# Queries and keys turned one row tile at a time in three self-attentions of a twelve-layer kernel

## The chip, the core and the metric

The kernel runs on one core of one Trainium2 chip, as one program of 42,986 instructions. The metric is the device time of a run in microseconds (us). Before the change three runs gave 1915.62, 1916.70 and 1917.58 us, median 1916.7.

## The reference, cut to what matters

The model has four blocks of cross-attention, self-attention and feed-forward over x (32 batches of 32 rows, 256 wide). Each layer gets a layer norm of x and is added to x. Three of the four self-attentions are touched; q, k and v have 16 heads of 16 columns, and a batch attends only within itself:

```python
# L0: softmax with a causal mask, interleaved rotation
q, k = rope(x @ W_Q), rope(x @ W_K)
out  = softmax(where(causal, q @ k.T / 4, -inf)) @ v @ W_O
# L2: 4 key/value heads; RMS norm of each head, then rotation, scores capped
q, k = rope(rms(x @ w_q)), rope(rms(x @ w_k))
out  = softmax(where(causal, 50 * tanh(q @ k.T / 4 / 50), -inf)) @ v @ w_o
# L3: sigmoid instead of softmax, heads of q and k divided by their length
q, k = l2norm(xn @ Wq), l2norm(xn @ Wk)          # xn: a second layer norm of x
out  = (sigmoid(15 * (q @ k.T - 0.29514)) * gate_q * gate_k) @ v @ Wo + bo
```

## The kernel before, in words

The 1024 rows are 8 row tiles of 128 (`NT = 8`), four batches each; 256 columns are two chunks of 128 (`C = 2`). Everything is float32. `PS` is PSUM, 8 banks of 512 columns. Layers run one after another; each is a block of five instruction streams, and each engine executes its own stream strictly in the written order, waiting on semaphores. The three stages are `l0_self` (line 2044, "softmax", tiles named l0a), `l2_self` (line 3398, "capped", l2a) and `l3_self` (line 3947, "resonance", l3a). All use the class `SelfAttention` (line 374).

**Preparation.** PE projects tile t to queries and keys (bank 4 + t % 2, line 419) and to values (bank 6 + t % 2, line 430). ACT copies them out (`copy_projections`, lines 501 and 488), and in l2a and l3a also writes squares (line 505) and takes the roots of their sums (line 496). DVE sums the squares (line 536), normalises and rotates: lines 760, 761, 771, 772 in l0a; 3461, 3463, 760, 761, 777, 778, 782, 783 in l2a; 4048, 4049, 4051 in l3a, where POOL multiplies by gates (line 4006) and DVE sums and applies them to the values (lines 4055, 4058).

**Turning.** `turn_tensor` transposes queries and keys of four row tiles into banks 0 to 3, one bank for each of two query and two key chunks. After each half ACT copies three banks (`turn_scalar`, lines 472 and 475) and DVE one (`turn_vector`, line 483), 512 columns at a time; keys are written twice, multiplied by one of two column masks. The second half waits until both have copied the first, since it uses the same banks. `keep_busy` (line 95) issues products of constants into bank 6 while PE would wait; their number is in `IDLE`.

**Attention.** Only then does `attend_tensor` start. For each row tile t:

- compare: PE, 64 instructions of 32 rows, scores to banks 0 to 3 (line 562). It waits until the scores of tile t - 1 have been read.
- softmax: DVE adds the mask and takes tops (lines 692, 698), POOL subtracts (673), ACT takes the exponential (628). capped: ACT tanh (622) and exponential (628), POOL masks (678). resonance: ACT sigmoid (634), POOL multiplies by a gate (678).
- DVE transposes the weights (714, `turn_probs`), ACT (and POOL) spread the values (615, 665), PE weighs them (576) into bank 4 + t % 2, DVE inverts and normalises (702, 708) or ACT copies (640), DVE transposes the rows (718, `turn_rows`), PE projects (585) into bank 6 or 7 by pairs of tiles, DVE adds each pair to X (737) and takes its moments.

PE's order is compare(t + 1), weigh(t - 1), proj(t - 2) for t = 0 to 9.

Of the kernel before, what the change touches and what calls it, by code (L numbers as in the profile page):

```python
# [14 lines left out]
ALU = mybir.AluOpType  # L15
# [3 lines left out]
P = 128  # L19
# [3 lines left out]
C = D // P  # L23
# [347 lines left out]
IDLE = {"l0a": (0, 0, 0, 0, 3, 0, 2, 0, 3), "l2a": (0, 0, 1, 3, 4, 2, 2, 2, 3), "l3a": (0, 0, 0, 0, 12, 0, 0, 3, 5)}  # L371


class SelfAttention:
# [10 lines left out]
    def __init__(self, core, es, name, kind, scale, kv_heads=16):  # L385
        self.core, self.name, self.kind, self.scale = core, name, kind, scale
        self.kv_heads, self.heads, self.width = kv_heads, 16 + kv_heads, (16 + kv_heads) * 16
        self.idle = IDLE[name]
# [15 lines left out]
        self.turned, self.half_copied_act, self.half_copied_dve = sem("turned"), sem("half_copied_act"), sem("half_copied_dve")  # L404
# [28 lines left out]
    def turn_tensor(self, pe, half):  # L433

        nc, PS = self.core.nc, self.core.PS
        if half:
            pe.wait_ge(self.v_copied, NT - 1)
            self.core.keep_busy(6, self.idle[4])
            pe.wait_ge(self.half_copied_act, 1)
            pe.wait_ge(self.half_copied_dve, 1)  # L440
        for t in range(4 * half, 4 * half + 4):
            if t % 4 and self.idle[t]:
                pe.wait_ge(self.v_copied, NT - 1)
                self.core.keep_busy(6, self.idle[t])
            pe.wait_ge(self.qk_rows, t + 1)
            for n, rows in enumerate((self.Q, self.K)):
                for c in range(C):
                    last = nc.tensor.transpose(PS[:, 2 * n + c, (t % 4) * P:(t % 4 + 1) * P], rows[:, t, c * P:(c + 1) * P], self.core.ident[:])
                    if t % 4 == 3:
                        last.then_inc(self.turned, 1)  # L450

    def project_tensor(self, pe, xT, wqk, wv):
# [8 lines left out]
        self.turn_tensor(pe, 0)  # L461
        self.turn_tensor(pe, 1)

    def half_of_keys(self, c, half, side):
        return self.K2[:, c, half * (B // 2):(half + 1) * (B // 2), side, :]

    def turn_scalar(self, act, half, side_of):

        nc, PS = self.core.nc, self.core.PS
        for c in range(C):  # L470
            act.wait_ge(self.turned, 4 * half + c + 1)
            nc.scalar.copy(self.QT[:, c, half * 512:(half + 1) * 512], PS[:, c, :])
        act.wait_ge(self.turned, 4 * half + 3)
        for side in range(2):
            last = nc.scalar.activation(self.half_of_keys(0, half, side), PS[:, 2, :].rearrange("p (b k) -> p b k", k=S), ACT.Copy, scale=side_of[:, side:side + 1])
        last.then_inc(self.half_copied_act, 1)

    def turn_vector(self, dve, half, side_of):

        nc, PS = self.core.nc, self.core.PS  # L480
        dve.wait_ge(self.turned, 4 * half + 4)
        for side in range(2):
            last = nc.vector.tensor_scalar(self.half_of_keys(1, half, side), PS[:, 3, :].rearrange("p (b k) -> p b k", k=S), side_of[:, side:side + 1], None, ALU.mult)
        last.then_inc(self.half_copied_dve, 1)
# [5 lines left out]
    def copy_projections(self, act, side_of, squares=None, size=None, second_half=None, values_from=0, **root):  # L490
# [7 lines left out]
        for t in range(NT):  # L498
# [14 lines left out]
            if t == NT - 2:  # L513
                self.turn_scalar(act, 0, side_of)
        if squares is not None:
            roots(NT - 1)
        self.turn_scalar(act, 1, side_of)
# [33 lines left out]
    def attend_tensor(self, pe, wo):  # L551
# [3 lines left out]
        def compare(t):  # L555
            if t:
                pe.wait_ge(self.scores_read, t)
# [22 lines left out]
        def proj(t):  # L580
            pe.wait_ge(self.out_copied, t + 1)
            if t % 2 == 0 and t >= 4:
                pe.wait_ge(self.added, t // 2 - 1)
# [10 lines left out]
        for t in range(NT + 2):  # L594
# [4 lines left out]
            if t >= 2:  # L599
                proj(t - 2)  # L600

    def attend_scalar(self, act, batch_of, gated=None):
# [39 lines left out]
        if self.kind == "capped":  # L642
            cap(0)
# [3666 lines left out]
```

## Time and profile before

| | |
|---|---|
| median of three runs | 1916.7 us (1915.62 to 1917.58) |
| the profiled execution | 1916.3 us, its span 1914.5 us |
| PE busy | 1792.7 us, 94% of the span |
| DVE, ACT, POOL busy | 1049.4, 847.6, 555.5 us |
| chain that ended last, by engine | PE 75%, DVE 11%, DMA 5%, issue 4%, ACT 3% |
| `keep_busy` of the whole kernel (line 95) | 320 records, 81.8 us on PE |

A page of the profile shows one execution. PE is the tensor engine's matrix products, PEld its weight loads, DVE, ACT and POOL are the vector, scalar and GpSimd engines. "PEclk" is the granted clock of the tensor engine as a share of 2.4 GHz. PE's busy time includes the products of `keep_busy`. A float32 product appears as two records or as four where it has two chunks.

### The profile page before, as it was taken

The numbers are of one execution on the slowest core, as the hardware profiler recorded it, in microseconds if no ns is written. First come the engines' busy times: TensorE is split into PE (matmuls) and PEld (weight loads), VectorE is DVE, ScalarE is ACT, GpSimd is POOL, SyncE is SP. The second block draws the span as 40 slices with busy tenths as digits, with TensorE's granted clock in tenths as the row PEclk, the third lists the DMA queues.
The fourth block names the chain that finished last, engine by engine and source line by source line (L and its number), as shares of the span: only waits on it lengthen the run. The fifth ranks groups of instructions, "written<-read, shape, count | busy, mean of one in ns | idle before, by whom it ended". The sixth has DMA issues, their size and how long they took to land.

```text
span 1914.5 us, 42986 instructions
## 1 busy us (share of the span) xinstructions
PE 1792.7 (94%) x16790; PEld 1384.6 (72%) x16790; DVE 1049.4 (55%) x2665; ACT 847.6 (44%) x2411; POOL 555.5 (29%) x596
## 2 busy tenths in 40 slices
PE   8999889999999989899999989999799899998998
PEld 6886569844766756699999967777544577766787
DVE  7787752252366438875555545556755555447411
ACT  6664541232266344334333335555511566635332
POOL 4441133100254203301222113332202465514242
PEclk9999889999999999999999999999999999998899
DMA  4221069570124110051899642111011455300397
GB/s 150 53 62 43 13 243 324 192 237 29 26 49 121 37 56 3 25 202 64 306 330 335 246 135 85 48 50 60 4 56 60 111 155 154 100 1 2 125 347 251
DMA packets 88303, 234.02 MB, mean 122 GB/s; under 512 B 10176, under 2 KB 45664, under 8 KB 81600
## 3 DMA queue, kind: packets, MB, share of 16 engines
q1 hardware_dynamic: 78416, 210.61, 33.0%
q0 software_dynamic: 5664, 15.47, 2.5%
q10 hardware_dynamic: 4048, 5.52, 0.9%
q8 instruction: 120, 1.97, 0.4%
q14 instruction: 55, 0.45, 0.1%
HBM read 216.35 MB, written 12.07 MB: 119 GB/s over the span
## 4 chain that ended last, share of the span: by engine, by line
PE 75%; DVE 11%; DMA 5%; issue 4%; ACT 3%; POOL 1%; SPq 0%; ACTq 0%; POOLq 0%; PEldq 0%; DVEq 0%; PEld 0%
PE PS L1137 15%; PE PS L1606 6%; PE PS L1148 5%; PE PS L3682 3%; PE PS L3502 3%; PE PS L3186 3%; PE PS L3707 3%; PE PS L3194 3%; PE PS L2402 2%; PE PS L2459 2%; PE PS L2761 2%; PE PS L2443 2%; PE PS L3219 2%; DMA l1x_probsT<-in_ctx_dram 2%; PE PS L2473 1%
## 5 line engine op out<-in xcount | busy, mean ns | idle before, releaser
L2361 POOL TENSOR_TENSOR l1x_probs<-l1x_probs,l1x_total 128x512 f32<-128x512 f32 x64 | 68.4, 1070 | 208.7 <-DVE l1x_total L2609 208.6
L1606 PE MATMUL PS<-weights,l0x_ctxT 128*128 128x256 f32 x512 | 121.0, 387 | 0.0
L1137 PE MATMUL PS<-l1f_xT,l1f_slot 128*128 128x128 f32 x1024 | 117.0, 275 | 0.0
L1137 PEld LDWEIGHTS PS<-l1f_xT,l1f_slot 128*128 128x128 f32 x1024 | 115.7, 192 | 0.1
L1606 PEld LDWEIGHTS PS<-weights,l0x_ctxT 128*128 128x128 f32 x512 | 94.6, 191 | 14.8 <-issue 2.1
L3156 POOL TENSOR_TENSOR l2x_probs<-l2x_probs,l2x_total 128x512 f32<-128x512 f32 x64 | 65.0, 1038 | 129.7 <-DVE l2x_total L3352 129.7
L95 PE MATMUL PS<-consts 128*128 128x256 f32 x320 | 81.8, 401 | 1.2
L1264 DVE SCALAR_TENSOR_TENSOR l1f_product<-PS,l1f_slot,l1f_side 128x128 f32<-128x128 f32 x128 | 36.0, 344 | 65.9 <-ACT l1f_side L1220 65.9
L3682 PE MATMUL PS<-l3x_keysT,l3x_QW 128*128 128x289 f32 x256 | 69.4, 415 | 1.7 <-issue 1.7
L95 PEld LDWEIGHTS PS<-consts 128*128 128x128 f32 x320 | 61.7, 201 | 12.3 <-issue 4.4
L1090 POOL DMA_INDIRECT l1f_out_dram<-l1f_out,l1f_sort_target_row x23 | 22.7, 986 | 159.5 <-DVE l1f_out L1247 159.5
L1220 ACT ACTIVATE l1f_side<-PS,l1f_slot 128x128 f32<-128x128 f32 x128 | 36.5, 368 | 66.0 <-PE PS L1137 66.0
L2534 ACT ACTIVATE l1x_probs<-PS,l1x_top 128x257 f32<-128x257 f32 x128 | 59.8, 475 | 6.8 <-DVE l1x_top L2604 4.4
L1786 ACT ACTIVATE l0x_sq<-PS 128x256 f32<-128x256 f32 x128 | 47.8, 385 | 33.3 <-PE PS L1606 33.2
L3707 PE MATMUL PS<-tagged,l3x_QT 128*128 128x256 f32 x256 | 60.6, 379 | 0.9 <-ACT tagged L3803 0.9
L3186 PE MATMUL PS<-l2x_ctxT,weights 128*128 128x257 f32 x256 | 61.1, 381 | 0.0
L2402 PE MATMUL PS<-HT,weights 128*128 128x512 f32 x128 | 55.9, 595 | 5.3 <-DVE l1x_AT L2572 5.3
L1137 PE MATMUL PS<-HT,weights 128*128 128x128 f32 x512 | 59.3, 276 | 1.5 <-DVE l1f_gated L1269 1.1
L3194 PE MATMUL PS<-weights,l2x_ctxT 128*128 128x256 f32 x256 | 60.4, 379 | 0.0
L1137 PEld LDWEIGHTS PS<-HT,weights 128*128 128x128 f32 x512 | 58.3, 192 | 2.7 <-DVE l1f_gated L1269 1.6
L1264 DVE SCALAR_TENSOR_TENSOR l1f_product<-PS,weights,l1f_side 128x128 f32<-128x128 f32 x120 | 33.8, 344 | 47.8 <-ACT l1f_side L1220 47.7
L3294 ACT ACTIVATE l2x_probs<-PS,l2x_top 128x257 f32<-128x257 f32 x128 | 59.2, 482 | 1.3 <-DVE l2x_top L3346 1.3
(661 smaller groups left out, 4583.7 us busy)
## 6 DMA issues: line engine op xcount, KB each, us to landing
l1f_slot<-in_experts_up_dram SPq DMA_DIRECT2D x16, 2056.0 KB, 9.9
weights<-in_experts_up_dram SPq DMA_DIRECT2D x8, 2056.0 KB, 10.2
l0f_slot<-in_experts_up_dram SPq DMA_DIRECT2D x15, 1024.0 KB, 7.9
weights<-in_experts_down_dram SPq DMA_DIRECT2D x21, 640.0 KB, 5.3
l1f_slot<-in_experts_down_dram SPq DMA_DIRECT2D x16, 640.0 KB, 4.5
l0x_ctxT<-in_ctxT_dram SPq DMA_DIRECT2D x32, 257.0 KB, 2.6
l2x_ctxT<-in_ctxT_dram SPq DMA_DIRECT2D x32, 257.0 KB, 2.7
l3x_ctxT<-in_ctxT_dram SPq DMA_DIRECT2D x32, 257.0 KB, 2.7
```

Source lines behind the costliest of these rows:

```text
L95: self.nc.tensor.matmul(self.PS[:, bank, 0:2 * P], self.ident, self.consts[:, 0:2 * P], start=True, stop=True)
L1137: done = nc.tensor.matmul(PS[:, bank + a, m * P:(m + 1) * P], mat[:, c, m * P:(m + 1) * P], x, start=(c == 0), stop=(c == 1))
L1148: done = nc.tensor.matmul(PS[:, 7, 0:D], self.hidden[j][:, m, :], w["down"][:, m, :], start=(m == 0), stop=(m == 3))
L1264: done = nc.vector.scalar_tensor_tensor(p[:, m, :], PS[:, 2 * u + 1, m * P:(m + 1) * P], w["b3"][:, 4 * u + m:4 * u + m + 1], self.side[u] ...
L1606: last = nc.tensor.matmul(PS[:, 2 * (b % 2) + k, half * D:(half + 1) * D], ctxT[b % SLOTS][:, c, half * P:(half + 1) * P], kw[:, c, k * D: ...
L2361: nc.gpsimd.tensor_tensor(p, p, bcast(total[b % 2][:, 2 * n:2 * n + 2], 2, KEYS), ALU.mult).then_inc(probs_done, 1)
L2402: done = nc.tensor.matmul(PS[:, 2 * (n % 2) + g, :], ff1[:, c, (g * HB + m) * P:(g * HB + m + 1) * P], core.HT[:, c, half * 512:(half + 1) ...
L3156: nc.gpsimd.tensor_tensor(p, p, bcast(total[b % 2][:, 2 * n:2 * n + 2], 2, 2 * P), ALU.mult).then_inc(probs_done, 1)
L3186: last = nc.tensor.matmul(PS[:, 4 + 2 * o, 0:CTX], wk[:, c, o * P:(o + 1) * P], ctxT[b % 2][:, c, :], start=(c == 0), stop=(c == 1))
L3194: last = nc.tensor.matmul(PS[:, 5, half * D:(half + 1) * D], ctxT[b % 2][:, c, half * P:(half + 1) * P], wv[:, c, :], start=(c == 0), stop ...
L3682: done = nc.tensor.matmul(PS[:, 2 * (b % 2) + u, 0:KEYS], QW[:, c, b, 4 * u:4 * u + 4, :].rearrange("p h q -> p (h q)"), keysT[b % 2][:, c ...
L3707: nc.tensor.matmul(PS[:, 6 + c, 0:2 * P], tokens[b % 2][:, half, c * P:(c + 1) * P], probsT[b % 2][:, half, :], start=(half == 0), stop=False)
```

## The change

Queries and keys are now turned one row tile at a time. All four transposes of a tile go side by side into bank 6, and ACT alone copies them out: one copy of 256 columns and two masked ones. PE turns three tiles before compare(0), ACT copies two before its attention begins. The other tiles are turned at the end of PE's turns of the attention loop, and copied at the start of ACT's. DVE prepares only `rows_ahead` tiles before its attention loop (6 in l0a, 4 in l2a and l3a) and one more at the end of each turn of the loop (`between`); in l3a POOL's gate products follow in the same way. The output projection has only bank 7, so that its next pair waits for the addition of the one before, and DVE's addition moves to the start of its turn. `keep_busy` of the turning phase is gone.

```diff
-IDLE = {"l0a": (0, 0, 0, 0, 3, 0, 2, 0, 3), "l2a": (0, 0, 1, 3, 4, 2, 2, 2, 3), "l3a": (0, 0, 0, 0, 12, 0, 0, 3, 5)}
+ROWS_AHEAD = {"l0a": 6, "l2a": 4, "l3a": 4}
+TURNS_AHEAD = 3
...
+    def turn(self, pe, t):
         nc, PS = self.core.nc, self.core.PS
+        if t == 0:
             pe.wait_ge(self.v_copied, NT - 1)
+        else:
+            pe.wait_ge(self.turn_copied, t)
+        pe.wait_ge(self.qk_rows, t + 1)
+        for n, rows in enumerate((self.Q, self.K)):
+            for c in range(C):
+                last = nc.tensor.transpose(PS[:, 6, (2 * n + c) * P:(2 * n + c + 1) * P], rows[:, t, c * P:(c + 1) * P], self.core.ident[:])
+        last.then_inc(self.turned, 1)
...
-        self.turn_tensor(pe, 0)
-        self.turn_tensor(pe, 1)
...
+    def copy_turned(self, act, t, side_of):
         nc, PS = self.core.nc, self.core.PS
+        act.wait_ge(self.turned, t + 1)
+        nc.scalar.copy(self.QT[:, :, t * P:(t + 1) * P], PS[:, 6, 0:2 * P].rearrange("p (c n) -> p c n", c=C))
+        keys = PS[:, 6, 2 * P:4 * P].rearrange("p (c b k) -> p c b k", c=C, k=S)
         for side in range(2):
+            last = nc.scalar.activation(self.K2[:, :, TB * t:TB * (t + 1), side, :], keys, ACT.Copy, scale=side_of[:, side:side + 1])
+        last.then_inc(self.turn_copied, 1)
...
         def compare(t):
+            pe.wait_ge(self.turn_copied, t + 1)
             if t:
                 pe.wait_ge(self.scores_read, t)
...
         def proj(t):
             pe.wait_ge(self.out_copied, t + 1)
-            if t % 2 == 0 and t >= 4:
-                pe.wait_ge(self.added, t // 2 - 1)
+            if t % 2 == 0 and t >= 2:
+                pe.wait_ge(self.added, t // 2)
             for c in range(C):
-                last = nc.tensor.matmul(PS[:, 6 + t // 2 % 2, ...
+                last = nc.tensor.matmul(PS[:, 7, ...
...
-        self.core.keep_busy(6, self.idle[NT])
-        pe.wait_ge(self.half_copied_act, 2)
-        pe.wait_ge(self.half_copied_dve, 2)
+        for t in range(TURNS_AHEAD):
+            self.turn(pe, t)
         pe.wait_ge(self.v_copied, NT)
         compare(0)
         for t in range(NT + 2):
...
             if t >= 2:
                 proj(t - 2)
+            if t + TURNS_AHEAD < NT:
+                self.turn(pe, t + TURNS_AHEAD)
...
+        for t in range(TURNS_AHEAD - 1):
+            self.copy_turned(act, t, side_of)
         if self.kind == "capped":
             cap(0)
         spread_values(0)
         for t in range(NT + 2):
+            if t + TURNS_AHEAD - 1 < NT:
+                self.copy_turned(act, t + TURNS_AHEAD - 1, side_of)
             if self.kind == "capped" and t + 1 < NT:
                 cap(t + 1)
...
         for t in range(NT + 3):
+            if t >= 4 and t % 2 == 0:
+                add(t // 2 - 2)
             if softmax and t < NT:
                 mask(t)
...
             if 0 <= t - 2 < NT:
                 turn_rows(t - 2)
+            between(t)
             if t >= 4 and t % 2 == 0:
                 j = t // 2 - 2
-                x = X[:, 2 * j:2 * j + 2, :]
-                dve.wait_ge(self.proj_done, 2 * j + 2)
-                nc.vector.tensor_tensor(x, PS[:, 6 + j % 2, :]...
                 dve.wait_ge(self.added, j + 1)
                 self.core.norm.take(dve, None, (2 * j, 2 * j + 1))
```

In `l2_self` DVE's preparation becomes (l3a alike, with `normalise_heads` and, one tile behind, `gate_values`; l0a has `rotate(t)` for six tiles, and the copy of the flipped second half after the third):

```diff
+            def rotate(t):
+                dve.wait_ge(at.rooted, t + 1)
+                dve_step(dve, nc.vector.reciprocal(size[:, t, :], size[:, t, :]))
...
+                rotation.products(dve, t)
+                rotation.combine(dve, t)
...
+            def between(t):
+                if t + at.rows_ahead < NT:
+                    rotate(t + at.rows_ahead)
...
+            for t in range(NT):
+                at.sum_squares(dve, t, squares, size)
+                if t % 2:
+                    rotate(t // 2)
+                elif t == 2:
                     flip.vector(dve, 1, core.HT)
```

## Rows read from the trace of the kernel before

**Rows 1.** Busy time by stretch, l2a and l3a: PE, PEld, DVE, ACT, POOL, clock, DMA.
```profile
1332.60:1398.10 65.50, 49.99 (x951) 37.69 (x950) 47.24 (x137) 38.33 (x92) 18.13 (x19) 0.94 0.10 34
1705.20:1776.50 71.30, 63.48 (x969) 44.44 (x969) 52.15 (x109) 42.65 (x94) 31.14 (x28) 0.90 0.01 2
```

**Rows 2.** Timeline of l0a: start, us, engine, line, operation, count [idle before <- releaser].
```profile
205.08 0.69 DVE L760 TENSOR_TENSOR l0a_cosines<-l0a_QK,weights 128x512 f32<-128x512 f32 x1 [0.62 <-ACT l0a_QK L501]
...
206.62 0.42 DVE L772 TENSOR_TENSOR l0a_QK<-l0a_cosines,l0a_sines 128x256 f32<-128x256 f32 x1
...
206.84 1.03 PE L430 MATMUL PS<-weights,HT 128*128 128x256 f32 x4
...
218.31 0.69 DVE L692 TENSOR_TENSOR l0a_scores<-PS,weights 128x512 f32<-128x512 f32 x1 [1.45 <-PE PS L562]
...
236.70 0.65 DVE L692 TENSOR_TENSOR l0a_scores<-PS,weights 128x512 f32<-128x512 f32 x1
...
239.32 0.69 DVE L737 TENSOR_TENSOR X<-PS,X 128x512 f32<-128x512 f32 x1
...
241.00 0.66 DVE L692 TENSOR_TENSOR l0a_scores<-PS,weights 128x512 f32<-128x512 f32 x1
...
248.07 0.45 DVE L718 STREAM_TRANSPOSE HT<-l0a_rows 128x256 f32<-128x256 f32 x1
```

**Rows 3.** Timeline of l2a.
```profile
1342.53 0.68 DVE L351 COPY HT<-PS 128x512 f32<-128x512 f32 x1
...
1349.03 0.55 PE L430 MATMUL PS<-weights,HT 128*128 128x64 f32 x4
...
1352.47 0.60 PE L448 MATMUL PS<-consts,l2a_QK 128*128 128x128 f32 x4
...
1356.20 0.26 DVE L3461 RECIPROCAL l2a_size<-l2a_size 128x20 f32<-128x20 f32 x1
...
1358.64 0.27 DVE L3461 RECIPROCAL l2a_size<-l2a_size 128x20 f32<-128x20 f32 x1
...
1368.61 0.62 ACT L628 ACTIVATE l2a_probs<-l2a_scores 128x512 f32<-128x512 f32 x1
...
1394.92 0.45 DVE L718 STREAM_TRANSPOSE HT<-l2a_rows 128x256 f32<-128x256 f32 x1
```

**Rows 4.** Timeline of l3a.
```profile
1729.22 1.03 PE L430 MATMUL PS<-weights,HT 128*128 128x256 f32 x4
...
1748.49 0.69 ACT L634 ACTIVATE l3a_probs<-PS,l3a_shift 128x512 f32<-128x512 f32 x1
...
1749.23 1.10 PE L562 MATMUL PS<-l3a_K,l3a_QT 32*32 32x64 f32 x64 [0.95 <-ACT l3a_probs L634]
...
1758.16 1.10 PE L562 MATMUL PS<-l3a_K,l3a_QT 32*32 32x64 f32 x64
...
1759.19 1.14 PE L576 MATMUL PS<-l3a_blocks,l3a_probsT 128*32 128x68 f32 x32
...
1760.26 2.08 PE L585 MATMUL PS<-weights,HT 128*128 128x256 f32 x4
...
1764.84 0.85 PE L562 MATMUL PS<-l3a_K,l3a_QT 32*32 32x64 f32 x64
...
1765.63 0.68 PE L576 MATMUL PS<-l3a_blocks,l3a_probsT 128*32 128x68 f32 x32
...
1766.24 1.13 PE L585 MATMUL PS<-weights,HT 128*128 128x256 f32 x4
...
1767.30 0.85 PE L562 MATMUL PS<-l3a_K,l3a_QT 32*32 32x64 f32 x64
...
1768.19 0.69 ACT L634 ACTIVATE l3a_probs<-PS,l3a_shift 128x512 f32<-128x512 f32 x1 [0.24 <-PE PS L562]
```

**Rows 5.** Instructions on l3a's keys: ns min/median/max, first and last start.
```profile
L475 ACT ACTIVATE l3a_K<-PS,weights x4: 698/701/702, 1732.7 to 1745.3; 128x512 f32<-128x512 f32 x4
```

**Rows 6.** Busy time by stretch in l3a's attention, columns as in rows 1.
```profile
1752.00:1756.00 4.00, 3.44 (x148) 2.64 (x128) 1.87 (x3) 3.21 (x7) 3.07 (x4) 0.50 0.03 8
```

More of the change, by code:

```diff
@@ L732, in attend_vector @@
                 turn_rows(t - 2)
+            between(t)
             if t >= 4 and t % 2 == 0:
                 j = t // 2 - 2
[L735 to L737 removed]
                 dve.wait_ge(self.added, j + 1)
@@ L4000, in _, with gate_products @@
             nc.gpsimd.tensor_tensor(core.X[:], core.X[:], bcast(bo, 1, NT), ALU.add).then_inc(biased, 1)
-            for t in range(NT):
+            def gate_products(t):
                 pool.wait_ge(at.qk_rows, t + 1)
@@ L4006, in _, with between @@
                 nc.gpsimd.tensor_tensor(four(products[t % 2][:]), four(at.QK[:, t, :]), bcast(gate, 2, 16), ALU.mult).then_inc(products_done, 1)
-            at.attend_gpsimd(pool, batch_of, factor=gates[:, :, 0:16], gated=gated)
+            def between(t):
+                if t + at.rows_ahead < NT:
+                    gate_products(t + at.rows_ahead)
+            for t in range(at.rows_ahead):
+                gate_products(t)
+            at.attend_gpsimd(pool, batch_of, factor=gates[:, :, 0:16], gated=gated, between=between)
         @block.scalar
@@ new lines, in gate_values, with between @@
+            def gate_values(t):
+                dve.wait_ge(products_done, t + 1)
+                nc.vector.reduce_sum(gates[:, t, :], products[t % 2][:].rearrange("p (h d) -> p h d", d=16), AX.X).then_inc(gates_done, 1)
+                dve.wait_ge(gates_done, t + 1)
+                dve.wait_ge(at.v_copied, t + 1)
+                nc.vector.tensor_tensor(at.values(t), at.values(t), bcast(gates[:, t, 16:32], 2, 16), ALU.mult).then_inc(gated, 1)
+            def between(t):
+                if t + at.rows_ahead < NT:
+                    normalise_heads(t + at.rows_ahead)
+                if t + at.rows_ahead - 1 < NT:
+                    gate_values(t + at.rows_ahead - 1)
@@ L4062, in _ @@
+            for t in range(NT):
+                at.sum_squares(dve, t, squares, size)
+                if t % 2:
+                    normalise_heads(t // 2)
+                    if t > 1:
+                        gate_values(t // 2 - 1)
             dve.wait_ge(biased, 1)
-            at.attend_vector(dve)
+            at.attend_vector(dve, between=between)
         flip.use += 1
```

130 lines of the change are left out of this document (35 added, 95 removed).

## Prediction

> **What bounds the kernel now.** I read busy time by stretch first [rows 1], then the timelines of the three stages, because a stage here is a chain and its shares do not tell which wait ends last. The reader is to see in [rows 1] that in 65.5 and 71.3 us PE looks busiest (49.99 and 63.48), but much of that is products of constants. What counts is when attention starts. In l0a PE has its last value product at 206.84 to 207.87, yet the first mask is added at 218.31 [rows 2]. In l2a the last value product ends at 1349.58 and the first exponential starts at 1368.61 [rows 3]. In l3a these are 1730.25 and 1748.49 [rows 4]. So 10, 19 and 18 us lie between projection and attention, bound by DVE's preparation of all eight tiles and by turning in two halves. After that a tile costs l0a 2.62 us of DVE (mask at 236.70 to the addition at 239.32), and 1.68 us more where a pair is added and its moments taken (239.32 to 241.00) [rows 2]; l3a costs 2.46 us of PE when its products are quick: compare 0.79, weigh 0.61, projection 1.06 (starts at 1764.84, 1765.63, 1766.24, 1767.30) [rows 4].
>
> **Prices.** A turn of one tile is four transposes, 0.60 us [rows 3]. The copy of a turned tile is three ACT instructions of 256 columns. No row shows that form; one of 512 with a mask takes 0.70 us [rows 5]. If time went by columns, three would take 1.05, if it did not fall at all, 2.1. I take 1.1, near the first, since the columns are halved. A round through bank 6 (turn, copy, both signals) is then 1.8 us, at most 2.8. ACT instead of six 512-column instructions each half (with DVE's two, moved to it) issues 24 small ones: DVE loses 2.8 us of work per stage, ACT gets some 4 more.
>
> **The start.** Turn(0) needs no more than tile 0 and six copied values, and follows the last value product at once. Compare(0) stands behind turn(2), so two rounds and 0.5 us after the first copy starts.
> l0a: first copy 208.2, compare(0) 211.7, first mask 212.5 against 218.31: 5.8 us earlier.
> l2a: DVE copies the flipped second half after tile 0's rotation but before the combination is interleaved with tile 1, at about 1341.0 instead of 1342.53 [rows 3], and PE waits for that copy, so all projections come 1.5 us earlier. Last values 1348.1; ACT's last square, DVE's sum and ACT's root 1.4 more: first copy 1349.5, compare(0) 1353.0. Tanh with its table, the spreading of tile 0 and copy(2) follow: first exponential 1357.1 against 1368.61, 11.5 us earlier.
> l3a: last values 1730.25, the same tail 1.2: compare(0) at 1735.0, sigmoid(0) at 1737.9 (spread, copy(2) and the table load before it) against 1748.49: 10.6 us earlier.
>
> **What the attention loops pay back.** Four things are added to each turn of the loop: DVE's preparation of a late tile, ACT's copy, PE's transposes, and the wait of the addition.
>
> l0a. Tiles 6 and 7 are rotated inside the loop, 2.0 to 2.1 us each (205.08 to 207.04 [rows 2]), on the engine that bounds it, although DVE idles from 205 to 212.5. Mask(2) comes at 220.1. Then DVE's addition stands at the head of turns 4, 6 and 8 and waits for weigh(t - 2) and proj(t - 3), with mask(t) queued behind it, and compare(t + 1) behind that. That is 1.3 us each with quick products (0.61 + 1.06 less the row transposition), of which the wait that DVE had anyway for the weighing takes about 0.4; in turn 4, when PE is slow and also has turn(5) ahead of compare(4), some 3.5. I schedule mask(4) at 229.8, mask(6) at 238.1, mask(7) at 241.6 against 241.00. The wait for the addition in turn 8 costs 0.6 more before the last row transposition (248.07). l0a: +1.2 us; -1 if PE is quick throughout, +4 if never.
>
> l2a. DVE prepares a tile in 2.44 us without the sum of squares (1356.20 to 1358.64 [rows 3]), 2.55 with combination right behind products. Rotate(4) is hidden, DVE being idle. Rotate(5), (6), (7) each stand ahead of the next inversion and transposition of weights. With 1.65 of its own work DVE then needs 4.2 us a tile: the inversions of tiles 0, 1, 2 come at 1362.2, 1366.4 and after add(0) at 1371.2. From there 1.7 a tile and 3.3 with an addition, with waits of 1.3 for the projection in turns 6 and 8. The last row transposition comes at 1387.0, 29.9 us after the first exponential, where it was 26.3 (1368.61 to 1394.92). So 11.5 less 3.6 is 7.9 us gained; I take 0.4 off for a slow projection, -7.5. The bounds are -8.5 and -4: ACT's order copy(t + 2), tanh(t + 1), exponential(t), spread needs 3.3 us, 4.3 by the upper price of a copy; when PE is slow throughout, PE needs about 5.2.
>
> l3a. Here a ring closes that the trace of before does not have. Copy(t + 3) stands ahead of sigmoid(t + 1) on ACT. It waits for turn(t + 3), which PE does last, behind compare(t + 1), weigh(t - 1) and proj(t - 2); and compare(t + 1) waits for sigmoid(t), as it did before (1749.23 right behind the end of the sigmoid of 1748.49 [rows 4]). All is serial: sigmoid 0.69, signal 0.05, PE 0.79 + 0.61 + 1.06, turn 0.65, copy until the next may start 1.0: 4.85 us with quick products. In [rows 6] the granted clock is 0.50, the 1.2 GHz level; there compare takes 1.03, weigh 1.07, projection 2.0 [rows 4], a turn perhaps 1.1, and the ring 7.0. Before, a tile took 2.46 and 4.1. The ring holds for sigmoids 1 to 5, the first two without all of PE's parts. Sigmoids at 1737.9, 1741.8, 1746.8, then 1753.8 with the slow ring. If it is quick from there, sigmoid(7) starts at 1767.6, if it alternates 1770.1, if slow to the end 1774; before 1768.19. In the middle, 1768.7. DVE's 3.0 us for a late tile and POOL's 3.3 lie beside the ring. At the end the addition ahead of the last transposition of weights adds about 1.5. l3a: +2.0 us; bounds -3.2 (quick throughout) and +7.
>
> **Clock.** [rows 6] follows two short compares with gaps between; the 1.2 GHz level came in all three stages at the start of attention and left once projections ran. With `keep_busy` gone and PE idle in each round, I assume the low level from the first compares until projections run, and both levels in turn in l3a's ring.
> The Trainium skill, page "TensorE: Matmul & The Clock Gate", section "HAM oscillation — how this bites in real kernels", has kernels whose bursts between waits each start at half clock; by that rule l3a's ring would alternate or stay low, l3a +2 to +7, and l2a's gain end nearer 6. The trace agrees so far as its 0.50 stands in such a stretch.
>
> Removed `keep_busy` and the other PE work shift nothing else: they lie in PE's waits. The stages behind start earlier by as much; weights for them are issued at the start of each stage and DMA's share there is 0.10 and 0.01 [rows 1].
>
> **Sum.** +1.2 - 7.5 + 2.0 = -4.3 us. The profiled execution took 1916.3, 0.4 below the median of 1916.7; 1912.0 on its base, 1912.4 on the median's.
>
> **Rivals.**
> 1. The ring and the slow clock win. PE at 1.2 GHz through most of the early turns: l3a +7, l0a +3, l2a -4: +6, 1922.7. For it: PE idles 1.65 us in a row in each quick ring (turn signal, copy, sigmoid), and the 0.50 of [rows 6]. Against: a projection and a turn in each ring, and projections brought the clock back before. It decides once l3a's ring exceeds about 6 us for all of sigmoids 3 to 5 and l2a gains under 6.
> 2. PE stays quick: l0a -1, l2a -8, l3a -3.2: -12, 1904.5. For it: transposes are full-width products and are now spread over the loop. Against: 1.2 GHz came before even with constants in the gaps.
> 3. The gains of the start are paid back to within the noise: l2a gains 5.5, l0a +1.5, l3a +2.5: -1.5, 1915.2. For it: each added wait is on the engine that bounds its stage. Against: l2a's 11.5 us of earlier start is large against 3.6 of longer loop.
>
> **How the numbers follow.** Measurement of this kernel can tell 0.2%, 3.8 us. The forecast (-4.3, range -8 to -1) has 0.40, rival 1 0.22, rival 2 0.13, rival 3 0.25. The forecast's own spread gives about 0.27 of its 0.40 to faster and 0.13 to the same; with 0.13 of rival 2 and 0.06 of rival 3 faster is 0.46. The same gets 0.13, 0.16 of rival 3 and nothing else, 0.29. Slower has rival 1 and 0.03 of rival 3, 0.25. The range 1905.5 to 1922 takes in rival 1 nearly whole and leaves out the far end of rival 2.
>
> **What would show it.** In the profile after: first mask of l0a near 212.5; first exponential of l2a 11 us after the stage's last values or less, and its last row transposition 7 to 8 us nearer to the stage's start; in l3a sigmoids 2 to 5 at distances of 4.8 to 7 us with ACT waiting for the transposes, where they had 2.5 to 4.1, and sigmoid(7) hardly moved; DVE waiting for the projection (its addition) in turns 4, 6 and 8. I am wrong if l3a's sigmoids keep under 4 us apart, if copies take 2 us, or if l2a's rows end less than 4 us earlier.

## The result and the profile after

The changed kernel takes 1922.25 us in the median of 14 runs (1918.17 to 1926.86), the kernel before 1915.66 in the median of 14 (1908.24 to 1919.62): a ratio of 1.0035, 95% interval 1.0022 to 1.0048, some 6.6 us slower. The forecast was 1912.4 with faster as the likeliest sign. The time lies at the far end of the range (1905.5 to 1922), a quarter of a microsecond past it, and within half a microsecond of rival 1, "the ring and the slow clock win" (1922.7, chance 0.22). The profiled execution took 1922.33 us, with a span of 1920.6 and a granted TensorE clock of 0.964, against 1914.5 and 0.979.

The stretches that answer to [rows 1] show most of it. The three windows are l0a, l2a and l3a of the kernel after; columns as in [rows 1].

```profile
182.50:257.25 74.75, 58.19 (x912) 39.95 (x913) 48.67 (x111) 40.36 (x91) 9.40 (x11) 0.77 0.11 36
1342.40:1405.80 63.40, 47.75 (x921) 35.98 (x920) 46.94 (x133) 42.59 (x109) 19.01 (x19) 0.81 0.10 36
1708.80:1786.35 77.55, 59.98 (x928) 40.99 (x928) 49.05 (x104) 45.46 (x110) 31.30 (x28) 0.80 0.01 2
```

The reader is to see that l3a is 6 us longer than in [rows 1] and that PE is busy for less of it (59.98 us against 63.48, which hold products of constants too), although each product now costs more: the granted clock fell from 0.90 to 0.80. In l2a it fell from 0.94 to 0.81.

To compare kernels whose stages start at different times, the table counts from each stage's entry, the first POOL copy into its tile of value blocks (in order 184.03, 1333.59 and 1705.90 before, 183.84, 1343.44 and 1709.57 after). "First" and "eighth" are the starts for tiles 0 and 7 of l0a's mask, l2a's exponential and l3a's sigmoid, "last add" the start of the stage's last addition to X. Each row is one profile; "again" marks a second execution of the same kernel, and E1 to E12 are told below.

```
                     l0a                        l2a                        l3a
              first eighth last add     first eighth last add     first eighth last add
before         34.3   57.0   65.7        35.0   55.6   63.0        42.6   62.3   69.0
before again   34.3   57.0   65.7        37.0   57.8   65.3        42.6   61.4   68.1
after          28.8   59.5   71.9        24.2   51.3   60.9        32.0   65.4   75.3
after again    27.6   57.7   67.3        24.4   51.9   60.6        32.0   65.8   75.6
E1 turn first  29.2   59.6   69.2        24.2   49.6   58.3        32.0   58.4   66.5
E2 8 rows l0a  28.9   55.4   67.9        24.4   51.8   60.5        32.0   66.5   76.0
E3 add back    28.8   56.5   65.6        24.5   51.4   59.7        32.0   67.2   73.8
E4 filled      28.8   58.1   69.9        24.0   52.7   61.4        32.0   59.3   67.4
E5 combined    28.9   54.0   62.8        24.4   50.9   58.7        32.0   56.6   64.8
E6 E5 filled   28.8   55.2   64.3        23.8   49.8   57.9        32.0   56.8   63.5
E7 one bank    34.3   61.5   71.2        37.1   57.9   67.6        42.6   62.5   70.6
E8 l2a only    34.3   57.0   66.7        24.0   51.1   60.8        42.6   60.1   66.8
E11 E5, filled
 l2a and l3a   27.8   52.9   61.6        23.9   49.8   57.9        32.0   56.9   63.6
E12 l0a only   27.4   57.6   70.0        38.2   58.9   66.3        42.6   61.0   67.7
```

In the first profiles l0a ends 6.2 us later, l2a 2.2 earlier, l3a 6.3 later, +10.3 in all; the unchanged code between and behind them gave about 4 back. The attentions do start where they were forecast. The loops are what went wrong.

**l3a's ring.** A timeline of one turn in the kernel after (start, us, engine, line, operation, idle before and its releaser), to be laid beside [rows 4]:

```profile
1750.59 0.70 ACT L614 ACTIVATE l3a_probs<-PS,l3a_shift 128x512 f32<-128x512 f32 x1
...
1751.43 1.09 PE L541 MATMUL PS<-l3a_K,l3a_QT 32*32 32x64 f32 x64 [1.87 <-ACT l3a_probs L614]
...
1752.45 1.14 PE L555 MATMUL PS<-l3a_blocks,l3a_probsT 128*32 128x68 f32 x32
...
1753.52 2.05 PE L564 MATMUL PS<-weights,HT 128*128 128x256 f32 x4
...
1755.39 0.61 PE L444 MATMUL PS<-consts,l3a_QK 128*128 128x128 f32 x4
1756.04 0.37 ACT L461 COPY l3a_QT<-PS 128x256 f32<-128x256 f32 x1 [3.28 <-PE PS L444]
1756.31 0.84 ACT L464 ACTIVATE l3a_K<-PS,weights 128x256 f32<-128x256 f32 x2
1757.03 0.70 ACT L614 ACTIVATE l3a_probs<-PS,l3a_shift 128x512 f32<-128x512 f32 x1
...
1763.50 0.70 ACT L614 ACTIVATE l3a_probs<-PS,l3a_shift 128x512 f32<-128x512 f32 x1
```

Sigmoid, compare, weigh, projection, transposition, copy, sigmoid: nothing overlaps, and once around this ring takes 6.44 us, the next time 6.47 and then 6.21. ACT stands idle 3.28 us for a transposition that itself took 0.61, because it is queued behind the weighing and projection on PE. PE idles 1.87 us for the sigmoid ahead of each comparison. The view of waits for the whole of l3a puts a sum on it (us in total, times, longest):

```profile
ACT l3a_QT L461 <- PE PS L444: 13.7, 6, 3.3
PE PS L541 <- ACT l3a_probs L614: 11.7, 6, 2.3
```

How the clock goes inside such a ring is seen in two windows of the next one, columns as above: the compare at the 2.4 GHz level, the projection 2 us later at the 1.2 GHz one. The third ring is alike: its compare takes 0.85 us from 1764.34, its projection 2.07 from 1765.76.

```profile
1757.80:1758.60 0.80, 0.73 (x64) 0.73 (x64) 0.58 (x2) 0.80 (x3) 0.79 (x1) 1.00 0.00 0
1759.60:1761.60 2.00, 2.00 (x10) 1.49 (x6) 1.97 (x3) 0.00 (x0) 1.44 (x2) 0.50 0.00 0
```

**l0a's additions.** The timeline of l0a after, to be laid beside [rows 2]:

```profile
212.65 0.69 DVE L677 TENSOR_TENSOR l0a_scores<-PS,weights 128x512 f32<-128x512 f32 x1 [8.19 <-PE PS L541]
...
214.15 1.42 POOL L657 TENSOR_TENSOR l0a_scores<-l0a_scores,l0a_top 128x512 f32<-128x512 f32 x1 [29.66 <-DVE l0a_top L683]
214.57 1.54 DVE L751 TENSOR_TENSOR l0a_sines<-l0a_QK,weights 128x512 f32<-128x512 f32 x1
...
221.36 0.68 DVE L677 TENSOR_TENSOR l0a_scores<-PS,weights 128x512 f32<-128x512 f32 x1
...
230.91 0.69 DVE L708 TENSOR_TENSOR X<-PS,X 128x512 f32<-128x512 f32 x1 [3.88 <-PE PS L564]
231.52 0.68 DVE L677 TENSOR_TENSOR l0a_scores<-PS,weights 128x512 f32<-128x512 f32 x1
...
239.19 0.69 DVE L708 TENSOR_TENSOR X<-PS,X 128x512 f32<-128x512 f32 x1 [1.51 <-PE PS L564]
...
243.31 0.66 DVE L677 TENSOR_TENSOR l0a_scores<-PS,weights 128x512 f32<-128x512 f32 x1
...
248.87 0.69 DVE L708 TENSOR_TENSOR X<-PS,X 128x512 f32<-128x512 f32 x1 [2.91 <-PE PS L564]
```

The first mask is at 212.65, forecast 212.5. From there DVE, which bounds this stage, waits 3.88, 1.51 and 2.91 us for projections, with the next mask queued behind the first two, and one product of a late tile's rotation takes 1.54 us where it takes 0.68 alone.

**l2a** has its first exponential 10.8 us nearer to its entry, and ends 2.2 nearer. Its timeline after, beside [rows 3]:

```profile
1367.63 0.65 ACT L608 ACTIVATE l2a_probs<-l2a_scores 128x512 f32<-128x512 f32 x1
...
1388.99 0.37 ACT L461 COPY l2a_QT<-PS 128x256 f32<-128x256 f32 x1 [3.08 <-PE PS L444]
...
1391.79 0.69 DVE L708 TENSOR_TENSOR X<-PS,X 128x512 f32<-128x512 f32 x1 [3.30 <-PE PS L564]
...
1401.83 0.45 DVE L703 STREAM_TRANSPOSE HT<-l2a_rows 128x256 f32<-128x256 f32 x1
```

From the first exponential to the last row transposition are 34.2 us, where the forecast had 29.9 and [rows 3] 26.3. The same two waits are in it that fill l3a and l0a: ACT for a transposition, DVE for a projection.

### The profile page after: what moved, and what is told of

It reads as the page before. It is cut to its first block, busy times and chain, and to the rows that moved or that the text cites. A ratio compares the mean times of both kernels' runs of the same rounds, so it can differ in the third digit from the quotient of the medians.

```text
span 1920.6 us, 42888 instructions
## 1 busy us (share of the span) xinstructions
PE 1787.3 (93%) x16700; PEld 1381.2 (72%) x16700; DVE 1046.0 (54%) x2653; ACT 858.6 (45%) x2459; POOL 555.9 (29%) x596
## 4 chain that ended last, share of the span: by engine, by line
PE 78%; DVE 10%; DMA 4%; issue 3%; ACT 3%; POOL 1%; SPq 0%; PEldq 0%; ACTq 0%; PEld 0%; POOLq 0%; DVEq 0%
PE PS L1127 16%; PE PS L1596 6%; PE PS L1138 6%; PE PS L3677 3%; PE PS L3179 3%; PE PS L3497 3%; PE PS L3702 3%; PE PS L3187 3%; PE PS L2395 2%; PE PS L2754 2%; PE PS L420 2%; PE PS L2452 2%; PE PS L2436 2%; PE PS L3212 2%; DMA l1x_probsT<-in_ctx_dram 2%
## 5 line engine op out<-in xcount | busy, mean ns | idle before, releaser
L1210 ACT ACTIVATE l1f_side<-PS,weights 128x128 f32<-128x128 f32 x120 | 34.2, 367 | 59.6 <-PE PS L1127 59.6
L95 PE MATMUL PS<-consts 128*128 128x256 f32 x230 | 58.1, 399 | 1.2
```

Of the source, the lines that this page charges most:

```text
L1210: nc.scalar.activation(self.side[u][:, m, :], PS[:, 2 * u, m * P:(m + 1) * P], ACT.Identity, bias=w["b1"][:, 4 * u + m:4 * u + m + 1]).the ...
```

## The experiments

Each was timed against the kernel before on the same chip, with 11 or 12 runs of its own, 6 in E5, E6 and E11, and a single one in E9 and E10. Differences "to after" are of medians, 1922.25; they come from two comparisons with the kernel before, so a difference of 3 us between two such kernels is not told from none. Places of single stages come from one profile each, and E9 and E10 show that these move by up to 4.6 us with no edit at all.

**E1, the transposition ahead of the weighing.** It takes apart the ring without changing what any instruction does.

```diff
                 compare(t + 1)
+            if t + TURNS_AHEAD < NT:
+                self.turn(pe, t + TURNS_AHEAD)
             if 1 <= t <= NT:
                 weigh(t - 1)
             if t >= 2:
                 proj(t - 2)
-            if t + TURNS_AHEAD < NT:
-                self.turn(pe, t + TURNS_AHEAD)
```

> The changed kernel with PE's turn of tile t + 3 right behind compare(t + 1), ahead of weigh(t - 1) and proj(t - 2). Theory of the ring (ACT's copy waits for a turn that PE does last in its turn of the loop): l3a's sigmoids 2 to 5, now 5.1 to 6.5 us apart, come to 3.5 to 4.2, l3a shortens by 6 us or more from stage entry to the last addition (75.4 now), l2a by 2 to 4 (60.9 now) since ACT no longer waits 3.4 and 3.1 us for transposes; l0a little (0 to 2 of 72.0), as DVE bounds it. In all 8 to 12 us less than the changed kernel, near or below the time before. Rival, the slow clock alone: PE is at 1.2 GHz in any order, compare and sigmoid stay serial with slow products, l3a gains under 3 us.

Measured: 1912.41 us (1906.62 to 1916.58), ratio to before 0.9981 (0.9966 to 0.9997); 9.8 us less than after. The timeline of its l3a:

```profile
1742.81 0.70 ACT L614 ACTIVATE l3a_probs<-PS,l3a_shift 128x512 f32<-128x512 f32 x1
...
1743.65 1.09 PE L541 MATMUL PS<-l3a_K,l3a_QT 32*32 32x64 f32 x64 [1.87 <-ACT l3a_probs L614]
...
1744.67 1.11 PE L444 MATMUL PS<-consts,l3a_QK 128*128 128x128 f32 x4
...
1745.82 0.37 ACT L461 COPY l3a_QT<-PS 128x256 f32<-128x256 f32 x1 [1.13 <-PE PS L444]
...
1746.82 0.70 ACT L614 ACTIVATE l3a_probs<-PS,l3a_shift 128x512 f32<-128x512 f32 x1
```

The ring is now sigmoid, compare, transposition, copy: 4.01 us, and 5.15 and 4.23 the next two times, although PE is at its slow level (the same compare in 1.09 us, the transposition in 1.11). ACT's wait for transpositions falls from 13.7 to 6.9 us, the eighth sigmoid comes 7.0 us sooner and l3a ends 8.8 sooner. The clock rose only from 0.80 to 0.84 (1709.00 to 1774.00). So at the slow level the order on PE's queue is worth 8.8 us in l3a. E4 takes the other factor, the level, at the old order.

**E2, all eight tiles of l0a rotated ahead.**

```diff
-ROWS_AHEAD = {"l0a": 6, "l2a": 4, "l3a": 4}
+ROWS_AHEAD = {"l0a": 8, "l2a": 4, "l3a": 4}
```

> The changed kernel, but in l0a DVE rotates all eight tiles before its attention loop (l2a, l3a as changed). If the late rotation on the bounding engine costs l0a its gain: the two rotations (2.9 and 2.5 us each in the loop, with DVE operations at 1.54 and 1.13 us beside POOL's) fit into the 8 us in which DVE waits for the first comparison, mask(2) comes 4 to 5 us earlier, l0a shortens from 72.0 to 67 to 69 us. Rival: PE at the 1.2 GHz level and the addition's wait (10.4 us in l0a) bound it, then the four us turn into longer waits for PE and l0a gains under 1.5 us.

Measured: 1918.75 us (1913.02 to 1922.90), ratio 1.0018 (1.0003 to 1.0032); 3.5 below after, with overlapping intervals. l0a ends at 67.9, between the two profiles of after (71.9 and 67.3), so the end of the stage doesn't tell it apart. What does is the third mask, at 34.1 us after the entry instead of 37.5 (3.4 earlier, where 4 to 5 were expected), the fourth, at 37.2 instead of 40.1, and the durations of the second product of the rotation (view of instructions by tile: ns min/median/max, first and last start), here and, below, in the kernel after:

```profile
L751 DVE TENSOR_TENSOR l0a_sines<-l0a_QK,weights x8: 682/684/686, 188.4 to 207.6; 128x512 f32<-128x512 f32 x8
```

```profile
L751 DVE TENSOR_TENSOR l0a_sines<-l0a_QK,weights x8: 676/684/1537, 188.4 to 219.9; 128x512 f32<-128x512 f32 x8
```

The longest of the after kernel's, 1.54 us, is that of a late rotation beside POOL's work; the two late rotations take 2.9 and 2.5 us in place of the 2.0 to 2.1 of the forecast. That the edit saves time in the whole kernel is not shown.

**E3, the addition back at the end of DVE's turn**, with the single bank kept.

```diff
         for t in range(NT + 3):
-            if t >= 4 and t % 2 == 0:
-                add(t // 2 - 2)
...
                 j = t // 2 - 2
+                add(j)
                 dve.wait_ge(self.added, j + 1)
```

> The changed kernel with DVE's addition back at its old place behind the transposition of rows (the projection keeps its single bank). If the addition at the head of the turn costs: DVE's wait for the projection (10.4, 6.6, 5.7 us in the three stages) falls to under 3 each, l0a shortens by 3 to 5 us and l2a by 2 to 3, 5 to 8 us in all. Rival: proj of the next pair now waits on PE for the later addition, with compare and turn behind it, and gives it back: under 2 us in all.

Measured: 1913.45 us (1910.68 to 1920.44), ratio 0.9990 (0.9973 to 1.0008); 8.8 us less than after. l0a ends at 65.6, where it does before (65.7), and DVE's wait there for projections falls from 10.4 us to this (view of waits):

```profile
DVE X L708 <- PE PS L564: 1.2, 2, 1.0
```

l3a keeps its ring (eighth sigmoid at 67.2) and ends only 1.4 sooner. E1 and E3 each remove one cost and leave the other. Of the 6.3 us in l0a the comparison of two single profiles may make up a part: the second profile of the kernel after ends l0a at 67.3 and not at 71.9.

**E4, constants multiplied where PE waited**, as the kernel before does, at the places of the new order.

```diff
+FILL = {"l0a": 2, "l2a": 2, "l3a": 3}
...
         for t in range(TURNS_AHEAD):
+            if t:
+                pe.wait_ge(self.v_copied, NT)
+                self.core.keep_busy(7, 2)
             self.turn(pe, t)
...
                 self.turn(pe, t + TURNS_AHEAD)
+                self.core.keep_busy(4 + t % 2, FILL[self.name])
```

> The changed kernel with products of constants on PE in the first two rounds (2 calls each, bank 7) and behind each turn of a tile in the attention loop (2 in l0a and l2a, 3 in l3a, into the free bank of the weighed rows). Theory of the clock: the granted clock of the three stages rises from 0.77, 0.81, 0.80 to over 0.9, PE's loop parts halve, l3a's sigmoids come 4.9 to 5.2 us apart instead of 6.4, in all 6 to 10 us less. Theory of the ring's order: the clock is part of it but fillers stand in front of the next comparison; l3a's ring stays above 4.8 us and the whole gains under 5 us; below 0 if the fillers run at 1.2 GHz and delay compare(t + 2).

Measured: 1915.68 us (1912.19 to 1928.59), ratio 0.9998 (0.9978 to 1.0017); 6.6 below after, as the theory of the clock had it. The window of its l3a, which starts 4.7 us ahead of the entry, has the clock at 0.98 (0.97 over the stage alone), and the ring closes in 4.83 us three times, as the forecast had it for quick products:

```profile
1704.00:1775.00 71.00, 62.39 (x982) 44.51 (x981) 50.45 (x111) 45.96 (x109) 31.38 (x28) 0.98 0.01 2
```

l3a ends 7.9 us sooner than after, l2a 0.5 later. With E1 this says that l3a's loss has two factors, products queued inside the ring and their slow level, and that taking away either one gives it back: 8.8 us by the order at a clock of 0.84, 7.9 by the clock at the old order.

**E5, E1 to E3 together**: the three edits shown above, and nothing else.

> The kernel after with three edits at once: turn(t + 3) between compare(t + 1) and weigh(t - 1), the addition of a pair back at the end of the turn, and all eight tiles of l0a rotated before its attention. Taken alone, against the kernel after, the first moved l3a's last addition by -8.8 us, l2a's by -2.6, l0a's by -2.7, the second by -1.4, -1.2 and -6.3, the third l0a's by -4.0. Theory (ring and head addition cost independent waits, each on its own stage): the sum holds within 2 us in l2a and l3a; l0a's two parts overlap, since both free VectorE. Last addition after the entry at l0a 62 to 64, l2a 57 to 58.5, l3a 65 to 66.5; whole kernel 1905 to 1909, that is 7 to 11 below the kernel before. Rival (the clock takes it back: what is ahead idles TensorE more): l3a stays at 68 or more and the whole is 1911 to 1914, no better than the first edit alone.

Measured: 1903.75 us (1901.72 to 1906.68), ratio 0.9931 (0.9915 to 0.9946), 12.9 us faster than before and 18.5 than after; better than the 1905 to 1909 expected. All three stages end in or within 0.2 us of the expected places (62.8, 58.7, 64.8). ACT's wait for transpositions in l3a is the last of what remains of the ring:

```profile
ACT l3a_QT L461 <- PE PS L444: 5.3, 5, 1.5
```

**E6, E5 with the products of constants ("fillers") of E4.** The expectation speaks of "7 before turns 1 and 2"; the edit is `keep_busy(7, 2)`, two products into bank 7.

> The previous kernel with filler products added on TensorE where it waited: 7 before turns 1 and 2 and 2 to 3 behind each projection of the first five turns of the loop. Theory that the granted clock is a cost of its own beside the ring: granted clock of the three stages over 0.88 (0.77 to 0.80 in the kernel after), l3a's last addition under 65 us after its entry, whole kernel 2 to 4 below the one without fillers. Theory that the order alone was the cost and the clock only follows: within 1.5 us of the one without fillers, l3a 65 to 67; l2a 0.5 to 1 later, since fillers there stand ahead of work that is ready.

Measured: 1904.48 us (1899.37 to 1906.81), ratio 0.9927 (0.9909 to 0.9945), the same as E5. The window of l3a has a clock of 0.97, where E5's has 0.87, and the stage ends 1.3 us sooner, l2a 0.8 sooner, l0a 1.5 later. Both kernels' windows, E5 first:

```profile
1697.40:1762.20 64.80, 53.60 (x924) 36.33 (x922) 47.37 (x101) 44.11 (x106) 31.37 (x28) 0.87 0.01 2
```

```profile
1703.00:1766.00 63.00, 57.99 (x956) 39.84 (x954) 46.09 (x95) 44.70 (x106) 30.83 (x25) 0.97 0.01 2
```

With the ring open, a tenth more clock goes with 1.3 us in l3a and nothing that the whole shows. Neither theory came out whole: the ends of l3a and l2a (63.5 and 0.8 sooner) are those of the first, that the clock is a cost of its own, and the whole is that of the second, that only the order was. A gain of 2 us, the least that the first one asked for, lies within what these runs can't tell; a gain of the size of E4's 6.6 is ruled out.

**E7, the single bank and the early addition put into the kernel before**, which turns by halves and rotates everything ahead.

```diff
-            if t % 2 == 0 and t >= 4:
-                pe.wait_ge(self.added, t // 2 - 1)
+            if t % 2 == 0 and t >= 2:
+                pe.wait_ge(self.added, t // 2)
...
-                last = nc.tensor.matmul(PS[:, 6 + t // 2 % 2, (t % 2) * D:(t % 2 + 1) * D], HT[:, c, t * P:(t + 1) * P], wo[:, c, :],
+                last = nc.tensor.matmul(PS[:, 7, (t % 2) * D:(t % 2 + 1) * D], HT[:, c, t * P:(t + 1) * P], wo[:, c, :],
...
         for t in range(NT + 3):
+            if t >= 4 and t % 2 == 0:
+                add(t // 2 - 2)
```

> The kernel before, with turning by halves kept, and only the projection's single bank and the addition at the head of turns 4, 6, 8 and 10 taken from the change. Theory that the addition's place costs by itself wherever the stage's loop is bound by VectorE: l0a 3 to 6 us later at its last addition (65.7 before), since its mask queues behind an addition that waits for the projection; l2a 0.5 to 2, l3a 0.5 to 2; whole kernel 4 to 9 above before. Theory that it costs only together with turns and late rotations in the loop: within 2 us of before in every stage, whole within 0.2%.

Measured: 1925.61 us (1920.14 to 1933.54), ratio 1.0041 (1.0026 to 1.0056), 9.0 us slower than before. l0a ends 5.5 us later, and its timeline shows where the time goes:

```profile
225.39 0.69 DVE L692 TENSOR_TENSOR l0a_scores<-PS,weights 128x512 f32<-128x512 f32 x1
...
232.50 0.69 DVE L723 TENSOR_TENSOR X<-PS,X 128x512 f32<-128x512 f32 x1 [4.00 <-PE PS L585]
233.11 0.68 DVE L692 TENSOR_TENSOR l0a_scores<-PS,weights 128x512 f32<-128x512 f32 x1
```

The fifth mask waits behind an addition that waits 4.00 us for the projection: 7.7 us from the fourth mask, where the kernel before has 4.0. With E3, which keeps the single bank and gets the time back, this names the addition's place, not the bank. The rest of the 9.0 us is in l2a and l3a, which end 4.6 and 1.6 us later than in the first profile of before, 2.3 and 2.5 later than in the second.

**E8, the change in l2a alone**, and **E12, in l0a alone**; the other two stages are those of the kernel before, each with its own class.

> The change in l2a alone; l0a and l3a as before. Theory that the stages add up: l2a's last addition 2 us nearer to its entry than the 63.0 of before (60.9), l0a 65.7 and l3a 69.0 within 0.5; whole kernel 1 to 3.5 below before. The forecast had 7.5 for this stage. Rival (the changed l0a and l3a cost something outside of their own loops, at the borders): 4 or more below before.

> The change in l0a alone; l2a and l3a as before. The change in l2a alone was -6.9 us. Theory that the stages add up: l0a's last addition at 71.9 us after the entry, l2a and l3a as before, whole 5 to 8 us above before; the remainder (+6.6 in all, +6.9 for l2a's part, less this) is then l3a's, 5.5 to 8.5. The forecast had +1.2 for l0a. Rival (l0a's slow clock is made up for by what follows): whole 0 to 3 above.

Measured: E8 1909.79 us (1903.16 to 1912.74), ratio 0.9962 (0.9947 to 0.9978), 6.9 us faster than before. E12 1920.18 us (1916.36 to 1930.61), ratio 1.0031 (1.0016 to 1.0046), 5.3 slower. By ratios, the kernel with l2a's change is at -7.3 us (-10.2 to -4.2), that with l0a's at +5.9 (+3.1 to +8.8), and what is left of after's +6.7 is put down to l3a: +8.1, by subtraction and not by a run of its own, and with the three intervals taken together anything from +3 to +13 by estimate.

E8 missed its expectation of 1 to 3.5 us below before and met the condition of the rival, 4 or more. Its profile does not put the whole of it into l2a. From l2a's entry to l3a's it takes 366.2 us, where the two profiles of before have 372.3 and 369.7 (3.5 to 6.1 less). From l3a's entry to the end, in code that is that of before, it takes 203.2, where they have 208.6 and 208.1 and E12 has 207.8. About 2 us of that lie in l3a, whose clock was 0.95 against 0.90 and 0.93. No run says whether the changed l2a brings these 5 us about or whether this one execution had them, so the -7.3 is what the edit is worth in the whole kernel, and l2a's own part is surer at 4 to 6.

**E9 and E10, the two kernels profiled a second time**, one execution each, no edit.

> A second profile of the kernel before, unchanged. In the first, 3.2 us fell to TensorE's slow clock right behind l2a's last addition (four products 128x512 of the router in 3.49 us from 1401.08), while the kernel after and the others had the same work at the fast one. Theory that this belongs to the kernel (TensorE was kept busy through the attention and fell only at its end): it recurs, and from l2a's last addition to l3a's first instruction there are again 309 us against 305 to 306 in the kernel after; so the whole of l2a's change is about -6, not -2. Theory that it is a matter of the single execution: it is gone, the stretch is at 305 to 306 and some other stretch has it.

> A second profile of the kernel after, unchanged. Theory that the sizes of the three stages belong to the kernel: last additions at 71.9, 60.9 and 75.3 us after the entries, each within 1.5. Theory that one execution's place of the slow clock makes them: they differ by 2 us or more, one down where another is up.

Measured: 1914.48 and 1918.26 us. The first products of the router behind l2a, in the first profile of before and then in the second (timeline):

```profile
1396.59 0.69 DVE L737 TENSOR_TENSOR X<-PS,X 128x512 f32<-128x512 f32 x1 [0.97 <-PE PS L585]
...
1401.08 3.49 PE L3502 MATMUL PS<-weights,HT 128*128 128x512 f32 x4
```

```profile
1400.14 0.69 DVE L737 TENSOR_TENSOR X<-PS,X 128x512 f32<-128x512 f32 x1 [0.97 <-PE PS L585]
1403.18 1.88 PE L3502 MATMUL PS<-weights,HT 128*128 128x512 f32 x4
```

The slow stretch behind the stage was a matter of the single execution, as the second theory had it. In the second profile the preparation of l2a has one (clock 0.91 against 1.00 from the entry to the first exponential), and that exponential comes 2.0 us later; in E7 and E12, whose l2a prepares in the same way, it comes 2.1 and 3.2 later. From l2a's entry to l3a's before is 372.3 and 369.7 us, after 366.1 and 365.0: l2a's change is worth 5.4 us between the means, near the 6 of E9's first theory though not for its reason, and inside the interval of E8. For E10, l2a and l3a repeat within 0.3 us; l0a does not (71.9 and 67.3), most of it behind the eighth mask, with the first mask 1.2 us earlier. l0a's size is better taken from E12.

**E11, E5 with fillers in l2a and l3a alone.**

> The three edits combined, with filler products in l2a and l3a and none in l0a. In the kernel with fillers everywhere l2a ended 0.8 and l3a 1.3 us sooner after their entries than without, l0a 1.5 later. Theory that stages add up: l0a 62.8, l2a 57.9, l3a 63.5, whole 2 us below the kernel without fillers, about 1901.5 if that is at 1903.75. Theory that the gain of the clock is within what one execution differs from another: whole within 1.5 us of 1903.75.

Measured: 1902.26 us (1900.69 to 1908.12), ratio 0.9934 (0.9917 to 0.9952). Stages end at 61.6, 57.9 and 63.6, as expected for the last two; the whole is 1.5 us below E5's, between the two theories. E5, E6 and E11 can't be told apart, and each beats both kernels by 0.7% and 1.0%.

## Why the prediction was wrong

The sign was wrong, and the step that failed is "What the attention loops pay back": the mechanisms were there, the sizes were not. Its l3a term was +2.0 us and the profile has +6.3; its l0a term was +1.2 and E12 has +5.9; l2a's loop pays back 7.9 us and not 3.6. Behind much of this stands one assumption, that PE leaves its slow level once projections run. Point by point:

- **The start** was right. Forecast 5.8, 11.5 and 10.6 us earlier; measured 5.5, 10.8 and 10.6. The copy of a turned tile, 1.1 us by estimate, took 1.0 (0.37, and 0.84 for the two masked ones, which overlap it; 1756.04 to 1757.03). Turn(0) waits for seven copied values (`v_copied`, NT - 1), not six; the first masks and sigmoids show no cost of it.
- **l0a, +1.2 us forecast, +5.9 measured (E12).** The masks of tiles 4, 6 and 7 came at 231.5, 239.8 and 243.3, all 1.7 us behind the schedule; some 1.3 of that is DVE beside POOL (0.86 and 0.45 above the 0.68 of an undisturbed product), which no term of the sum had. Most of the rest came in turn 8, where the addition waited 2.91 us instead of 1.3, since the projection ahead of it ran at the slow level (2.08 us at 246.75, twice the quick one), and behind it, where the last addition comes 2.8 us after the last row transposition instead of 1.7. The forecast had the mechanism and priced the wait as slow in turn 4 only. E3 gives back all of l0a's loss, E7 makes one of 5.5 us in the kernel before.
- **l2a, -7.5 forecast, -7.3 measured (E8).** That the number came out is luck. The profiles have 2.2 us in the stage and 5.4 from its entry to l3a's, and part of E8's gain lies behind l3a's entry. The loop pays back 7.9 us, not 3.6, as l3a's ring and the slow additions are in l2a too (three waits of ACT of up to 3.4 us, three of DVE of up to 3.3). Against that the kernel before itself loses 2 to 5 us to the slow clock: in the first profile behind this stage (308.6 us from the end of its last addition to l3a's entry, against 303.7 in the second and 304.6 and 303.8 in the kernel after), which [rows 3], ending before that, can't show, and in the second in its preparation.
- **l3a, +2.0 forecast, +6.3 in the profile, +8.1 left by E8 and E12.** The ring was described instruction by instruction and its two prices were near (4.85 quick, measured 4.83 in E4; 7.0 slow, measured 6.2 to 6.5). Counted from the entry, the first four sigmoids were forecast at 32.0, 35.9, 40.9 and 47.9 us and came at 32.0, 36.0, 41.0 and 47.5. What failed is "in the middle, 1768.7", which is 62.8 after the entry, between rings that are all quick from there and rings that alternate (64.2): the eighth sigmoid came at 65.4. Three slow rings followed each other (1750.59, 1757.03, 1763.50, 1769.71), although in the second and third the compare was quick: the level fell again ahead of the projection. At the end the stage paid 2.8 us more behind the eighth sigmoid (7.9 against 5.1 to the last row transposition), not 1.5.
- **The clock.** The slow level was assumed until projections run; it came back in all three stages (projections of 2.08, 1.73 and 2.05 us at 246.75, 1386.37 and 1753.52, where a quick one takes 1.13), whose means are 0.77, 0.81 and 0.80. The rule of the Trainium skill cited above, page "TensorE: Matmul & The Clock Gate", section "HAM oscillation — how this bites in real kernels", would have given +2 to +7 for l3a by the prediction's own working; the profile's +6.3 agrees with its upper half. In the manner the trace differs from that section, whose bursts start cold behind each wait: in the second and third ring the compare right behind PE's wait of 1.87 us ran quick (0.87 and 0.85 us), and the level fell inside the burst (projections 2.08 and 2.07). [rows 4] already showed a whole slow turn in the middle of the loop (1.10, 1.14 and 2.08 us from 1758.16), where PE had no ring to wait for; a ring in which it waits 1.87 us should have been priced as at least as slow.

Rival 1's point of decision, that the ring exceeds about 6 us for sigmoids 3 to 5 and l2a gains under 6, was met in its first half; l2a gained more in the timed runs than it allowed (-7.3, where it had -4) and l0a lost more (+5.9, not +3), so its total of 1922.7 is right with two terms off against each other. Rival 2, PE quick throughout, is what E4 tried to force: even with a clock of 0.98 in l3a, and 0.88 and 0.92 in l0a and l2a, the kernel is no faster than before. Rival 3's direction, the start paid back in the loops, held, but its l0a and l3a terms (+1.5, +2.5) were as much too small as the forecast's. A run with the change in l3a alone is missing, so l3a's size in the whole rests on subtraction.

## What to carry to other kernels

When work is moved into a loop, put it on each engine's queue by how soon its result is waited for, and follow the order once around: one transposition queued behind two products that nobody yet waited for closed a ring through two engines (9.8 us between E1 and after), and one addition moved to the head of a turn made the next tile's first step wait for the projection of an earlier pair (8.8 and 9.0 us, E3 and E7). Keeping the clock up gave 6.6 us while PE's products were in such a ring, and 1.3 us in its stage once the ring was open. A stage's gain is not to be read from its own window in one profile: l2a's was 2.2 us there, 5.4 from stage to stage over two profiles, and 7 in timed runs of the whole.

## What the runs showed of the hardware

- Two tensor operations, one on DVE and one on POOL, both reading two tiles of SBUF, did not overlap where these traces have them together. In the rows of l0a above, DVE's product of 214.57 takes 1.54 us, which is 0.68 and a wait to about 215.4, near the end of POOL's at 215.57; POOL's started at 214.15 under the DVE product before it and took 1.42 instead of 1.05. It recurs at 218.84: DVE's product takes 1.13 us, to 219.97, beside POOL's, which ends at 219.43. A DVE transposition, which reads one tile, takes its usual 0.70 us at 223.01 beside POOL's of 222.84. The Trainium skill, page "SBUF — State Buffer", section "SBUF: two separate sides", says that the two share one pair of ports, which whichever starts first holds for its whole instruction when DVE has two SBUF inputs; the trace agrees.
- ACT's instruction of 256 columns with a mask takes 0.48 us in l3a after where one of 512 takes 0.70 ([rows 5]): halving the columns saves 0.22, a third.
- A second execution of the same kernel put the 1.2 GHz level elsewhere (behind l2a in one, in its preparation in the other) and moved single stages by 2 to 4.6 us, while the whole moved by 1.8 us (before) and 4.1 (after).
